# Probabilities of an attention kernel turned through HBM: two of four heads before, all four after

## The reference, cut to what matters

```python
x = x + attn(cond(x, ...), ...)                 # stage 1: 32 heads of 16, causal
x = x + ffn(cond2(x, ...), ...)                 # stage 2: cond2; stage 3: ffn with a low-rank part
# cond2: 8 batches, 8 groups, 4 query heads of 128 for each group, 128 tokens
q, k, v = x @ Wq.T, x @ Wk.T, x @ Wv.T          # RMS norm and rotary embedding on q and k
k_all = concat([k_cache, k]); v_all = concat([v_cache, v])      # 512 cached keys and 128 new ones
probs = softmax(mask(q @ k_all.T * SCALE))      # 128 x 640 for each head
out = (probs @ v_all) @ Wo.T                    # summed over all heads
```

## Time and profile before

| what | value |
|---|---|
| time, median of 3 executions | 1300.29 us (1300.09 to 1301.01) |
| the profiled execution, first to last instruction | 1299.0 us |
| stage 2, slots 0 to 63 | about 250 to 1255 us |
| PE / DVE / ACT / POOL busy, share of the span | 96% / 76% / 64% / 64% |
| DMA queue of SP | 189.64 MB, 51.2% of 16 engines |

### The profile page before, as it was taken

One profiled execution on the slowest core, in us unless ns is written; L12 is line 12 of the kernel. 1 busy time (PEld: TensorE's weight loads), 2 busy tenths in 40 slices (PEclk: granted clock), 3 DMA queues, 4 the chain that ended last, 5 costly groups with the idle time before them and its releaser, 6 DMA issues. The chain is left out here.

```text
span 1299.0 us, 26260 instructions
## 1 busy us (share of the span) xinstructions
PE 1249.3 (96%) x7496; PEld 1074.6 (83%) x7496; DVE 985.6 (76%) x2388; ACT 837.8 (64%) x2505; POOL 836.1 (64%) x787
## 2 busy tenths in 40 slices
PE   5799997799999999999999999999999999999988
PEld 4677775688888888888888888888888888888878
DVE  3567857467888878887888778878888888788766
ACT  2667777466767676666766776676666767666731
POOL 1656656475767676758665876687667766775741
PEclk9899998899999999999999999999999999999999
DMA  7546554345455555555555555555555455455441
GB/s 264 204 170 243 206 217 151 104 115 146 133 139 134 140 140 142 143 139 134 146 136 146 137 144 131 139 137 144 134 143 140 131 143 143 126 138 141 134 133 65
DMA packets 288945, 191.48 MB, mean 147 GB/s; under 512 B 151201, under 2 KB 256674, under 8 KB 287778
## 3 DMA queue, kind: packets, MB, share of 16 engines
q1 hardware_dynamic: 287792, 189.64, 51.2%
q10 hardware_dynamic: 1010, 0.17, 0.1%
HBM read 143.60 MB, written 79.69 MB: 172 GB/s over the span
## 5 line engine op out<-in xcount | busy, mean ns | idle before, releaser
L1779 POOL TENSOR_TENSOR b_p_l<-b_moved,b_p_h 128x640 fp32r<-128x640 f32 x128 | 200.9, 1570 | 163.9 <-PE ps L1375 93.8
L1514 ACT ACTIVATE b_pf<-b_sm,b_mn 128x640 f32<-128x640 f32 x256 | 212.4, 830 | 127.5 <-DVE b_mn L1624 127.5
L1624 DVE CUSTOM_DVE_ANT_0 b_sm<-ps,mask_row,b_rstd 128x640 f32<-128x640 f32 x256 | 225.0, 879 | 53.7 <-PE ps L1301 48.8
L1526 ACT ACTIVATE b_p_h<-b_moved 128x640 fp32r<-128x640 f32 x128 | 94.7, 740 | 160.0 <-DMA b_moved<-blocks_of_probs 158.8
L1660 DVE SCALAR_TENSOR_TENSOR b_hacc<-ps,b_ri,b_hacc 128x512 f32<-128x512 f32 x248 | 182.4, 736 | 4.6 <-PE ps L1301 4.3
L1299 PE MATMUL ps<-b_w_h,x1t_h 128*128 128x512 f32 (+1 forms) x512 | 178.8, 349 | 0.1
L1299 PE MATMUL ps<-b_kt_h,b_qt_h 128*128 128x320 f32 x512 | 169.5, 331 | 4.6 <-DVE b_mn L1624 4.2
L1300 PE MATMUL ps<-b_w_l,x1t_h 128*128 128x512 f32 (+1 forms) x512 | 173.4, 339 | 0.0
L1301 PE MATMUL ps<-b_w_h,x1t_l 128*128 128x512 f32 (+1 forms) x512 | 173.2, 338 | 0.0
L1301 PE MATMUL ps<-b_kt_h,b_qt_l 128*128 128x320 f32 x512 | 159.3, 311 | 0.0
L1300 PE MATMUL ps<-b_kt_l,b_qt_h 128*128 128x320 f32 x512 | 159.2, 311 | 0.0
(11 more groups left out here) (177 smaller groups left out, 3371.1 us busy)
## 6 DMA issues: line engine op xcount, KB each, us to landing
blocks_of_probs<-b_blk SPq DMA_DIRECT2D x128, 320.0 KB, 2.4
b_moved<-blocks_of_probs SPq DMA_DIRECT2D x512, 80.0 KB, 2.1
kv_of_batch<-in_kv SPq DMA_DIRECT2D x128, 256.0 KB
b_ck<-kv_of_batch SPq DMA_DIRECT2D x64, 256.0 KB, 4.0
b_cv<-kv_of_batch SPq DMA_DIRECT2D x256, 64.0 KB, 1.9
raw<-in_w SPq DMA_DIRECT2D x32, 384.0 KB, 3.2
raw<-in_wo SPq DMA_DIRECT2D x32, 256.0 KB, 2.8
a_xt<-in_xt SPq DMA_DIRECT2D x8, 256.0 KB, 6.7
```

Of the source, the lines that this page charges most:

```text
L1514: act.activation(pf[:, h % 2], sm[:, h % 2], ACT.Exp, bias=mn[:, m.b % 2, h:h + 1], scale=-1.0, accum_out=rs[:, m.b % 2, h:h + 1]).then_in ...
L1526: act.activation(blocks_of(p_h[:, :, h * P:(h + 1) * P]), moved[:, d].rearrange("p (a t j) -> p a t j", a=LT, j=QUAD), ACT.Copy).then_inc( ...
L1624: dve.tensor_tensor_reduce(sm[:, h % 2], score_row, mask_row[:, m.b], rstd[:, m.b % 4, h:h + 1], -MASKED, ALU.add, ALU.min, mn[:, m.b % 2, ...
L1779: pool.tensor_tensor(blocks_of(p_l[:, :, h * P:(h + 1) * P]), moved[:, d].rearrange("p (a t j) -> p a t j", a=LT, j=QUAD), blocks_of(p_h[: ...
```

## The change

All four heads take the way through HBM. `turn_probs` on PE, `low` on DVE and the copy from PSUM on ACT are gone. The two PSUM banks that held the turned probabilities become a second pair of score banks, so `scores(m, h)` waits only for `minima` of the head two before. `blocks_back` becomes one DMA of 128 partitions: keys stand on the partitions in another order (key `j` of block `c` on partition `4j + c`), and the new keys and the cached values are stored in this order too. `blk` still has two places, `moved` has four. On POOL the rotary sum and the norm of the new key (`rope_keys`) are gone: the sum goes to DVE (`key_sum`), the norm to ACT (`turned_key`). Some small tiles share memory with others now (`low`, `small_rows`, a bfloat16 `squares_out`), which moves no work.

```diff
             def blocks_back(m, h):
 
-                d = BY_DMA.index(h)
-                sp.wait_ge(blk_out[d], 16 * (m.n + 1))
-                wait(sp, ml_sb, len(BY_DMA) * (m.n - 1) + d + 1)
-                for c in range(LT):
-                    rows_of = blocks_dram[d].rearrange("(a i) (c n) -> c i a n", a=LT, c=LT)[c]
-                    sp.dma_start(moved[c * QUAD:(c + 1) * QUAD, d].rearrange("p (a n) -> p a n", a=LT), rows_of).then_inc(moved_in[d], 16)
+                sp.wait_ge(blk_out[h], 16 * (m.n + 1))
+                wait(sp, ml_sb, REP * (m.n - 1) + h + 1)
+                rows_of = blocks_dram[h].rearrange("(a j) (c n) -> (j c) a n", a=LT, c=LT)
+                sp.dma_start(moved[:, h].rearrange("p (a n) -> p a n", a=LT), rows_of).then_inc(moved_in[h], 16)
 
             def slot(m, one, two, last):
-                if m:
-                    blocks_away(m, 0)
-                    blocks_back(m, 0)
-                    blocks_away(m, 1)
+                blocks_away(m, 0)
+                blocks_back(m, 0)
+                blocks_away(m, 1)
                 if two:
                     key_rows(two)
                 blocks_back(m, 1)
-                if two:
-                    value_rows(two)
                 if m.b in (2, 3, 4, 5):
                     chunk(m.g + 1, m.b - 2)
                 if m.b in (6, 7) and m.g + 1 < G:
...
                 if m.b == 0 and m.g > 0:
                     chunk(m.g, KT + 2)
                     chunk(m.g, KT + 3)
+                blocks_away(m, 2)
+                blocks_away(m, 3)
+                blocks_back(m, 2)
+                blocks_back(m, 3)
+                if two:
+                    value_rows(two)
...
-                wait(pe, mn_sb, REP * m.n + h)
+                wait(pe, mn_sb, REP * m.n + h - 1)
...
-                turn_probs(m, 2)
                 if two:
                     project_q(two)
...
-                turn_probs(m, 3)
...
+            def turned_key(m):
+                act.wait_ge(kab2_sb, m.n + 1)
+                act.wait_ge(rstd_sb, m.n + 1)
+                act.activation(ka[:], kb[:], ACT.Copy, scale=rstd[:, m.b % 4, REP:REP + 1]).then_inc(kr_sb, 1)
+
...
                 exponent(m, 2)
                 if m.b == 6:
                     kv_weights(m.g + 1)
-                high_moved(m, 0)
+                high(m, 0)
+                if one:
+                    turned_key(one)
                 if last:
                     output(last)
                 exponent(m, 3)
-                high(m, 2)
+                high(m, 1)
                 if one:
                     new_keys(one)
                     cache_values(one)
-                high_moved(m, 1)
+                high(m, 2)
                 if m.n == end.n - 1:
                     h_out(act, 0)
                 if two:
...
+            def key_sum(m):
+                dve.wait_ge(kab_sb, m.n + 1)
+                dve.tensor_tensor(kb[:], ka[:], kb[:], ALU.add).then_inc(kab2_sb, 1)
+
...
-                if last:
-                    low(last, 3)
+                if before:
+                    accumulate(before, 3)
                 minima(m, 2)
                 turn_blocks(m, 1)
-                if before:
-                    accumulate(before, 3)
+                if one:
+                    key_sum(one)
...
                 minima(m, 3)
+                turn_blocks(m, 2)
                 if last:
                     output(last)
                     invert(last)
-                low(m, 2)
+                turn_blocks(m, 3)
...
             def slot(m, one, two, last):
                 if one:
                     rms(one)
-                    rope_keys(one)
+                if last:
+                    low_probs(last, 3)
...
-                low_moved(m, 0)
+                low_probs(m, 0)
+                low_probs(m, 1)
                 if one:
                     cache_values(one)
-                low_moved(m, 1)
                 if two:
                     rope_queries(two)
+                low_probs(m, 2)
```

More of the change, by code:

```diff
@@ L516, in slot @@
                 if b == LAST:
+                    next_turned_key(Item(0, 0))
                     next_queries(Item(0, 0))
@@ L932, in phase3 @@
     ht_h, ht_l = (x1t_l[:, 4], x1t_l[:, 5]), (x1t_l[:, 6], x1t_l[:, 7])
-    b_gate = sb("b_gate", [P, NR])
-    first = sb("first", [P, NR])
+    b_gate, first = small_rows[:, 0:NR], small_rows[:, NR:2 * NR]
+    sc, weight = [small_rows[:, 8 * (1 + i):8 * (2 + i)].rearrange("p (k r) -> p k r", k=2) for i in range(2)]
+    top, expert = small_rows[:, 24:26], small_rows[:, 26:28]
     most = sb("most", [P, 2, MAXR])
[L936 to L940, removed]
     lowt = sb("lowt", [P, 2, P], F32R)
@@ L948, in phase3 @@
     bth_sb, btl_sb = sem("bth_sb"), sem("btl_sb")
-    small = ((b_gate, "b_gate"), (first, "first"), (most, "most"))
+    small = ((b_gate, "b_gate"), (first, "first"), (most[:], "most"))
     def flat(ap):
@@ L1496, in cache_values @@
                 act.activation(v_h[:, m.b % 2], cv[:], ACT.Copy).then_inc(vch_sb, 1)
[L1498 to L1502 removed]
             def exponent(m, h):
                 act.wait_ge(mn_sb, REP * m.n + h + 1)
[L1506 to L1511 removed]
+                wait(act, blk_sb, REP * m.n + h - 1)
                 if h == 0:
@@ L1579, in slot @@
                     exponent(one, 0)
-            scalar_first(act, (q_weights, kv_weights, squares, new_kv, queries, cache_keys, new_keys, cache_values))
+            scalar_first(act, (q_weights, kv_weights, squares, new_kv, queries, turned_key, cache_keys, new_keys, cache_values))
             slots(act, slot)
@@ L1710, in low_kv_weights @@
                 dve.tensor_tensor(w_l[:, :, cols], raw[:, :, cols], w_h[:, :, cols], ALU.subtract).then_inc(wkvl_sb, 1)
-            vector_first(dve, (rope_products, new_values, queries, new_keys, minima, low_weights, low_kv_weights))
+            vector_first(dve, (rope_products, new_values, key_sum, queries, new_keys, minima, low_weights, low_kv_weights))
             slots(dve, slot)
             accumulate(end.before(), 2)
-            low(end, 3)
             accumulate(end.before(), 3)
@@ L1808, in _ @@
             pool.wait_ge(const_sb, 1)
-            gpsimd_first(pool, (q_weights, kv_weights, rope_queries, rms, rope_keys, cache_keys, cache_values))
+            gpsimd_first(pool, (q_weights, kv_weights, rope_queries, rms, cache_keys, cache_values))
             slots(pool, slot)
+            low_probs(end, 3)
             pool_ffn(pool)
```

127 lines of the change are left out of this document (46 added, 81 removed).

## The result

The kernel after takes 1538.75 us (median of 4 executions, 1535.0 to 1545.33), the one before 1300.19 us beside it (1298.98 to 1301.01). The ratio is 1.1831, interval 1.1798 to 1.1863: 18% slower. The forecast was 1450 us with a range to 1510. The sign and the place are as forecast, the size is not: +239 us instead of +150.

The account below looks back on a forecast made before the run. PE was taken to bound the kernel; the change replaces it by a ring through head 2's round trip, mean 18.1 us a slot against 15.72. 2.35 us more in 64 slots, 150 us, gives 1450 us, range 1290 to 1510.

Parts of the forecast that it names:

- the ring through head 1: Kernel before: loop from head 1's write through its copy and the exponent to its next turn, 15.66 us, just one slot.
- What PE gains: Transposes of heads 2 and 3 leave PE: 1.00 us a slot, 64 us in all; a slot of 14.72 us if PE-bound.
- The mechanism: On ACT exponent(one, 0) stands behind high(m, 2), which waits for head 2's round trip: a ring averaging 18.1 us a slot.
- I take 0.93 + 1.26 + 0.37 = 2.56 us from the issue to ACT: Head 2's read as one DMA: start of bytes, transfer at full use, then the following issue; bounds 2.2 and 3.3 us.
- From the read of head 1 to the read of head 2, 4.60: Ring's queue part: head 1's read, the piece of weights and head 2's write one behind the other; mean over b.
- 2.59 from the write of head 1 to its read: Issue of head 1's write to issue of its read, with something queued behind the write: 2.59 us.
- Transfers overlap, so that the queue adds nothing: Rival: ring through head 2 is 15.1 to 16.0 us a slot; 1279 to 1334 us, likeliest near 1305; chance 0.14.
- PE stays the bound: Rival: PE still sets the pace in stage 2, so the kernel is faster, 1236 to 1275 us; chance 0.08.
- the trip of head 2 with the queue in front: Deciding sign, head 2's write issue to its copy: 7.3 us queued, 4.73 undisturbed; PE sets the pace only under some 4.3.
- PE's clock falls: Rival: idle PE drops to the low clock for half of each slot, about 1550 us; worse than 1510 has chance 0.10.
- rope_keys ... nothing on the path: Removing rope_keys from POOL gains 0 to 1 us of POOL and nothing on the path.
- the term it could have lengthened: Ring's last stretch, from exponent(one, 0) along DVE's order to the next turn of head 1: 5.4 us.

Follow-up runs that it names:

- the last kernel of the table: Kernel after with orders redone on ACT, POOL and SP, rope_queries(two) earlier on POOL, and 80 KB transfers instead of 320: 1282.93 us, 0.9848.
- the kernels with 80 KB: Each probability write and read moves 80 KB instead of 320: on the kernel after 1346.05 us (1.0328), on the one with orders redone 1282.93 us (0.9848).
- the fastest kernel of this kind at 320 KB: Kernel after with orders redone on ACT, POOL and SP, and POOL's rope_queries(two) ahead of low_probs(m, 1) and cache_values(one): 1414.05 us, 1.0852.

## Why the prediction was right in kind and wrong in size

**What bounded the kernel before.** Right: PE. That the ring through head 1 is level with it is right for b = 5, where it was read. The kernel with weights ahead of that head's read shows it near for b = 0, 6 and 7 too, and about 1 us of air for b = 2 to 4.

**What PE gains.** Right, and of no use. The floor forecast as 14.72 us was measured as 14.57 where nothing else was in the way (15.72 less 1.15, with 1.00 forecast), and 64 slots at the floor would be the 1236 us of the rival: the last kernel of the table is 1283, and its two long slots cost 8 x (2.6 + 3.7) = 50.

**The mechanism.** Right. Head 2's round trip stands ahead of `exponent(one, 0)` in ACT's list, which closes a ring. The exponent follows `squares` directly, ACT waits longest at head 2 (246.1 of 420.2 us), and more work on PE changes nothing. But it was told as the only ring, and that was too simple: with head 2's copy out of it the slot was still 17 to 19.6 us in most b, by the next copy in the list and by SP's own order.

**The step that failed** is the cost of the transfers, and in it three terms:

- *"I take 0.93 + 1.26 + 0.37 = 2.56 us from the issue to ACT"*: measured 3.27, at the upper bound of 3.3. The estimate was too low even for a read with the queue nearly to itself. Head 0's read has no other issue for 2.07 us behind it (median), and its data land 2.71 us after the issue at the least, 2.86 in the median; the sum had it at ACT in 2.56. So 0.3 of the 0.7 us is the read itself, as one DMA of 128 partitions. Head 2's read has a median of 3.07 and a mean of 3.26: most are near head 0's, and some last over 4 us, as the one shown (870.46 to 874.89). The read of head 3, issued 0.8 us behind, doesn't explain these: in the 8 slots in which it comes 1.6 us or more behind, head 2's needs 3.1 to 5.0.
- *From the read of head 1 to the read of head 2, 4.60*: measured 5.49. The prediction took the piece of weights and one write through the queue. But the read of head 1 that stands in front needs longer than the sum gave it (a mean of 3.44 us to land), the write of head 3 follows head 2's by some 0.5 us, and the windows from 866 to 870.5 us have all three and the weights.
- *2.59 from the write of head 1 to its read*: measured 2.83, with `key_rows` behind it.

Head 0's read in the slot shown, and its copy 2.94 us later (timeline of all engines):

```profile
860.24 0.37 SPq L1254 DMA_DIRECT2D b_moved<-blocks_of_probs  x1
...
863.18 0.74 ACT L1501 ACTIVATE b_p_h<-b_moved 128x640 fp32r<-128x640 f32 x1 [0.69 <-DMA b_moved<-blocks_of_probs]
```

0.7 + 0.9 + 0.2 less 0.3 of the two last terms make the 1.5 us between 18.1 and 19.6; 64 x 1.5 = 96 us cover the 89 us between 1450 and 1539. What the three have in common is that the sum priced each transfer by how it goes nearly alone, and laid them in a row. On this queue the same 320 KB take other times beside other transfers: in the kernel after, the write of head 0 lands in 2.17 us (median), that of head 2 in 4.20. The Trainium skill says of one queue of a DMA engine ("DMA: Bandwidth & Descriptors", section "Two DMAs through the same engine are not ordered") that descriptors start in order but are pipelined. The traces agree that transfers mix, and show no gain from it at 320 KB: the three windows above have 1217 KB in 4.5 us, 270 GB/s, where the earlier trace rows has 328 for a write.

Which neighbour lengthens which transfer stays open. The kernel with the weights last speaks against the one behind: in 48 of its slots the write of head 2 is issued under 0.6 us behind the read of head 1, with nothing between them, and it lands in 3.9 us (median) in the 13 in which head 3's write comes 1.8 us or more later, in 4.0 in the 31 in which that comes after 1.2 to 1.8. There the read ahead is enough. That volume as a whole has a large share, the kernels with 80 KB show (2.83, 5.49 and 3.27 became 1.97, 4.43 and 2.10).

**The other rivals.** *Transfers overlap, so that the queue adds nothing* (1279 to 1334): no run has it at 320 KB; at 80 KB, where the queue adds little, the ring is 16.5 us. *PE stays the bound*: only with both causes gone. (The prediction gives 7.3 us for the trip of head 2 with the queue in front; its own times, 4.1 to 10.77, make 6.7. Measured are 7.31.) *PE's clock falls*: it did, in 21 of 61 slots and for one run of products, but the mean granted clock of stage 2 is 0.94, not the half of each slot that would make 1550, and the slots in which it happened are not longer than others of the same b. That the time came out near this rival's number is no evidence for it. The Trainium skill tells of kernels whose products start slow after each wait for a DMA ("TensorE: Matmul & The Clock Gate", section "HAM oscillation — how this bites in real kernels"): the trace agrees in part, since it happens in 21 of 61 slots here, and it does not lengthen them.

**The small terms.** *"rope_keys ... nothing on the path"* was wrong in the kernel before, where the move as a whole costs 15 us, and wasn't tried alone in the one after, where the term it could have lengthened is shorter than forecast (5.22 for 5.4). `key_sum` takes 0.25 us in the median and 0.36 in the mean, where 0.2 was taken. Slots are shortest at b = 1, as forecast (18.17), and longest at b = 0 (20.86); b = 5 is 20.05, and b = 6 at 20.82 was not forecast as long: there POOL has the weights too, which was named as a risk and left out of the sum. The DMA share is 0.63 and not 0.7, because the slot became longer than forecast.

What stays open is how the rest of the orders' share divides among ACT, POOL and SP: they were moved one after the other, not each alone.

## What to carry to other kernels

Work taken off the bounding engine counts only until the next ring: before trading it for round trips through memory, follow one loop from a copy to the next slot's same copy through every in-order list, SP's included, and price each transfer by one that has as much beside it, not by one that goes nearly alone. A first ring taken away shows a second one that was nearly as long; a run with small transfers and all instructions in place tells in one step how much of a loss is volume. And a reordering on SP or ACT that puts a load last puts it first in the next slot.

## What the runs showed of the hardware

- The landing of a 320 KB write depends on what else is in the queue more than on the write. In the kernel after it is 2.17 us for head 0 and 4.20 for head 2 (medians). Over all heads it is 2.4 us in the kernel before and 2.7 in the one after, 3.5 and 3.7 with the copies on ACT late, and 3.9 in the fastest kernel of this kind at 320 KB; at 80 KB it is 1.7 to 1.9. Each better order on ACT and POOL made these writes slower.
- A read of 320 KB as one DMA brought its data earlier than four of 80 KB when little was beside it: 2.86 us from the issue, against 3.34 from the first issue to the last landing (medians of head 0, after and before). Each of the four lands 2.1 us after its own issue, but they are issued one after the other, 1.74 us in all. Over all heads the one DMA takes 3.2 us.
- A move of 0.39 us of work a slot onto ACT and 0.25 us onto DVE cost 15 us in 64 slots, though ACT was busy only 67% of stage 2 and DVE 80%, and POOL was relieved.
